# An attention block's instruction order on TensorE: scores ahead of the next rows' transposition; key, values, query in this order

## What is computed

```
x = x + tanh(g_xattn[l]) * attention_l(layernorm(x), ctx, ctx)     # l = 0..3
    scores = Q K^T / sqrt(8);  p = softmax(scores);  out = (p V) Wo + bo
x = x + tanh(g_ffn[l]) * ffn_l(layernorm(x))
```

## Time and profile before

| what | value |
| --- | --- |
| median of 3 runs | 1207.94 us (1206.35 to 1207.98) |
| the profiled execution's own time | 1206.75 us |
| its span, first to last instruction | 1204.6 us |
| PE, DVE, ACT, POOL busy | 78%, 75%, 58%, 44% of the span |
| mean granted TensorE clock over the span | 0.883 of full speed |

### The profile page before, as it was taken

The page is one execution under the profiler, slowest core; times in us unless marked ns, Lnnn a source line. Parts: engine busy times, 40 slices in busy tenths (PEclk is TensorE's granted clock), DMA queues, the critical chain, the costliest instruction groups (busy, mean ns, idle before and its releaser), DMA issues.

```text
span 1204.6 us, 29852 instructions
## 1 busy us (share of the span) xinstructions
PE 936.0 (78%) x11473; PEld 727.7 (60%) x11491; DVE 908.8 (75%) x2195; ACT 693.3 (58%) x1807; POOL 525.5 (44%) x646
## 2 busy tenths in 40 slices
PE   4999979989988860899789999677799998233332
PEld 3888869968876650466377777433488886122221
DVE  3888877857877672566478888688677786999997
ACT  3887754357766620345367777565477876444442
POOL 4444412235477767222478886155523331122222
PEclk9999989999999965899899999788899999556665
DMA  7830000000000001464101100000000000000000
GB/s 203 267 106 2 3 2 2 2 1 2 2 19 25 24 29 48 138 194 140 44 28 28 29 28 20 1 1 1 1 2 2 2 2 2 5 14 13 10 13 17
DMA packets 60526, 44.41 MB, mean 37 GB/s; under 512 B 15197, under 2 KB 55782, under 8 KB 59367
## 3 DMA queue, kind: packets, MB, share of 16 engines
q1 hardware_dynamic: 54996, 33.96, 9.5%
q0 software_dynamic: 4096, 8.34, 2.3%
q10 hardware_dynamic: 1298, 0.27, 0.1%
HBM read 23.73 MB, written 18.87 MB: 35 GB/s over the span
## 4 chain that ended last, share of the span: by engine, by line
issue 38%; PE 30%; DVE 23%; SPq 5%; ACT 2%; POOL 1%; DMA 1%; DVEq 0%; POOLq 0%; another core or an unknown queue 0%; ACTq 0%
PE ps L518 5%; PE ps L547 5%; DVE rowmax L1399 3%; DVE sm L1404 3%; PE ps L585 3%; PE ps L655 2%; PE ps L646 2%; PE ps L647 2%; DVE q_b L1628 2%; DVE q_s L1608 2%; DVE q_r L1619 2%; DVE hT L1598 2%; DVE q_r L1627 2%; PE ps L442 1%; DVE q_r L1566 1%
## 5 line engine op out<-in xcount | busy, mean ns | idle before, releaser
L1399 DVE TENSOR_REDUCE rowmax<-ps 128x16 f32<-128x1024 f32 x128 | 156.7, 1224 | 98.5 <-PE ps L547 98.1
L773 ACT ACTIVATE pr<-ps 128x512 f32<-128x512 f32 x256 | 152.8, 599 | 37.1 <-PE ps L518 35.8
L1404 DVE TENSOR_TENSOR sm<-ps,rowmax 128x1024 f32<-128x1024 f32 x128 | 156.7, 1224 | 3.4
L518 PE MATMUL ps<-cst,sm 128*128 128x128 f32 x1024 | 139.3, 280 | 21.6 <-DVE sm L1404 21.4
L585 PE MATMUL ps<-vbd,pr 128*64 128x18 f32 x4096 | 147.4, 215 | 2.2 <-ACT pr L773 2.2
L585 PEld LDWEIGHTS ps<-vbd,pr 128*64 128x64 f32 x4096 | 134.8, 139 | 15.3 <-ACT pr L773 2.8
L1008 POOL TENSOR_SCALAR xn<-x_sb,mv_all,rstd_all 128x128 f32<-128x128 f32 x128 | 102.2, 799 | 81.4 <-PE ps L524 79.4
L518 PEld LDWEIGHTS ps<-cst,sm 128*128 128x128 f32 x1024 | 113.1, 142 | 31.2 <-DVE sm L1404 30.2
L803 ACT ACTIVATE vbd<-ps 64x128 f32<-64x128 f32 x256 | 71.0, 277 | 92.6 <-PE ps L571 90.4
L807 ACT ACTIVATE qbd<-ps,bqp,cst 128x128 f32<-128x128 f32 x256 | 104.5, 463 | 7.0 <-PE ps L571 3.7
L1075 POOL TENSOR_TENSOR q_out<-q_b,q_s 128x1280 bf16<-128x1280 bf16 (+2 forms) x18 | 38.1, 2119 | 137.5 <-DVE q_b L1629 137.5
(11 more groups left out here) (244 smaller groups left out, 2374.6 us busy)
## 6 DMA issues: line engine op xcount, KB each, us to landing
slots<-hT SPq DMA_DIRECT2D x8, 1024.0 KB, 10.7
sm<-slots SPq DMA_DIRECT2D x32, 256.0 KB, 3.2
expert_out<-xn_all SPq DMA_DIRECT2D x16, 256.0 KB, 2.9
ew<-in_L_ffn_w SPq DMA_DIRECT2D x24, 128.0 KB, 2.5
out<-x_sb SPq DMA_DIRECT2D x32, 64.0 KB, 1.5
slots<-xn_all,row_s POOLq DMA_INDIRECT x64
big<-expert_out,row_g POOLq DMA_INDIRECT x64
x_sb<-in_x SPq DMA_DIRECT2D x1, 512.0 KB, 6.5
```

Source lines behind the costliest of these rows:

```text
L518: last = nc.tensor.transpose(bank(y, b)[:, r * P:(r + 1) * P], sm[y][:, c:c + P], ident)
L773: nc.scalar.activation(pr[y][:, b, :], bank(y, b), ACT.Exp, scale=SCALE).then_inc(p_ready[y], 1)
L1399: v.tensor_reduce(row3, sc, AX.X, ALU.max).then_inc(rowmax_ready[x], 1)
L1404: v.tensor_tensor(sm[x][:, :].rearrange("p (r g k) -> p r g k", r=RG, k=S), sc, row3.unsqueeze(3).broadcast_to([P, RG, 4, S]), ALU.subtrac ...
```

## The change

In TensorE's half the scores of new and the transposition of the output of old come directly behind the eight transpositions; the context or router transposition and that of the rows of ahead come behind them. Then follow the key of ahead, the weight preparation or the router's product, the values of new (now into bank 1 of y, behind the wait for the second exponential), the query of ahead and the products with the probabilities. The wait for `xnT_ready` moves to just ahead of the query; the waits of the output's transposition for `xnT_ready`, `ctxT_ready` and `rT_ready` are gone. ScalarE takes both exponentials first, then waits for the output's, the context's or router's and the rows' transposition, copies the rows, the context or router rows and the output, then the values, and waits for key and query only behind them. VectorE's and GpSimd's programs are not edited.

```
--- before.py
+++ after.py
@@ -517,25 +517,17 @@
                                 c = (2 * r + b) * P
                                 last = nc.tensor.transpose(bank(y, b)[:, r * P:(r + 1) * P], sm[y][:, c:c + P], ident)
                             last.then_inc(smT_psum[y], 1)
-                    if ahead is not None:
-                        if prev is None and k > 0:
-                            pe.wait_ge(x_done[y], IT * k)
-                        pe.wait_ge(xn_ready[y], IT * k + ahead + 1)
-                        nc.tensor.transpose(bank(y, 3)[:, 0:P], xn[y][:, :], ident).then_inc(xnT_psum[y], 1)
-                    if l == 0:
-                        turn_context(t, y)
-                    if l == 1:
-                        turn_routed(t, y)
-                    if old is not None:
-                        pe.wait_ge(o_ready[x], IT * l + old + 1)
-                    if oldest is not None:
-                        pe.wait_ge(x_done[y], IT * k + oldest + 1)
                     if l == 1:
                         reuse_routing_bank(t, x)
                     if new is not None:
                         if prev is not None:
                             pe.wait_ge(v_taken[y], IT * l + prev + 1)
                         pe.wait_ge(k_ready[x], IT * l + new + 1)
+                    if oldest is not None:
+                        pe.wait_ge(x_done[y], IT * k + oldest + 1)
+                    if old is not None:
+                        pe.wait_ge(o_ready[x], IT * l + old + 1)
+                    if new is not None:
                         if l == 1:
                             for r in range(RG):
                                 rows = slice(r % 2 * S, (r % 2 + 1) * S)
@@ -548,27 +540,20 @@
                                                         kT[x][rows, :, b * S:(b + 1) * S], start=(l != 1), stop=True, skip_group_check=True)
                         last.then_inc(s_psum[x], 1)
                     if old is not None:
-                        if ahead is not None:
-                            pe.wait_ge(xnT_ready[y], IT * k + ahead + 1)
-                        if l == 0 and turned_context(t) is not None:
-                            pe.wait_ge(ctxT_ready, turned_context(t) - FIRST + 2)
-                        if l == 1 and routed(t + 1) is not None:
-                            pe.wait_ge(rT_ready[y], routed(t + 1) // NS + 1)
                         nc.tensor.transpose(bank(y, 3)[:, P:2 * P], o_sb[x][:, :], ident).then_inc(oT_psum[x], 1)
-                    if prev is not None:
-                        pe.wait_ge(p_ready[y], 2 * (IT * l + prev) + 1)
-                    if new is not None:
-                        for b in range(2):
-                            for a in range(2):
-                                cols = wv[l][:, :].rearrange("d (r a w) -> d a r w", a=2, w=2 * HD)[:, a, :, :]
-                                dst = bank(y, 0)[a * S:(a + 1) * S, 2 * P + b * S:2 * P + (b + 1) * S].rearrange("p (r w) -> p r w", r=RG)
-                                last = nc.tensor.matmul(dst, ctxT[:, t * P + b * S:t * P + (b + 1) * S], cols, start=True, stop=True, skip_group_check=True)
-                        last.then_inc(v_psum[x], 1)
+                    if l == 0:
+                        turn_context(t, y)
+                    if l == 1:
+                        turn_routed(t, y)
                     if ahead is not None:
-                        if old is None:
-                            pe.wait_ge(xnT_ready[y], IT * k + ahead + 1)
-                        nc.tensor.matmul(bank(y, 0)[:, P:2 * P], wq[l][:, :], xnT[y][:, :], start=True, stop=True)
-                        nc.tensor.matmul(bank(y, 0)[:, 0:P], wk[l][:, :], ctxT[:, (ahead * NS + y) * P:(ahead * NS + y + 1) * P], start=True, stop=True).then_inc(kq_psum[y], 1)
+                        if prev is None and k > 0:
+                            pe.wait_ge(x_done[y], IT * k)
+                        pe.wait_ge(xn_ready[y], IT * k + ahead + 1)
+                        nc.tensor.transpose(bank(y, 3)[:, 0:P], xn[y][:, :], ident).then_inc(xnT_psum[y], 1)
+                    if ahead is not None:
+                        if prev is not None:
+                            pe.wait_ge(p_ready[y], 2 * (IT * l + prev) + 1)
+                        nc.tensor.matmul(bank(y, 0)[:, 0:P], wk[l][:, :], ctxT[:, (ahead * NS + y) * P:(ahead * NS + y + 1) * P], start=True, stop=True)
                     if l == 0:
                         prepare_weights(t, y)
                     if l == 1:
@@ -576,6 +561,17 @@
                     if prev is not None:
                         pe.wait_ge(v_taken[y], IT * l + prev + 1)
                         pe.wait_ge(p_ready[y], 2 * (IT * l + prev) + 2)
+                    if new is not None:
+                        for b in range(2):
+                            for a in range(2):
+                                cols = wv[l][:, :].rearrange("d (r a w) -> d a r w", a=2, w=2 * HD)[:, a, :, :]
+                                dst = bank(y, 1)[a * S:(a + 1) * S, 2 * P + b * S:2 * P + (b + 1) * S].rearrange("p (r w) -> p r w", r=RG)
+                                last = nc.tensor.matmul(dst, ctxT[:, t * P + b * S:t * P + (b + 1) * S], cols, start=True, stop=True, skip_group_check=True)
+                        last.then_inc(v_psum[x], 1)
+                    if ahead is not None:
+                        pe.wait_ge(xnT_ready[y], IT * k + ahead + 1)
+                        nc.tensor.matmul(bank(y, 0)[:, P:2 * P], wq[l][:, :], xnT[y][:, :], start=True, stop=True).then_inc(kq_psum[y], 1)
+                    if prev is not None:
                         for r in range(RG):
                             for h2 in range(2):
                                 for b in range(2):
@@ -775,7 +771,10 @@
                 def half(t, x, fetch, further, later, ahead, new, prev, old, oldest):
                     y = 1 - x
                     if prev is not None:
-                        exponentials(y, 0, 2 * (IT * l + prev) + 1)
+                        for b in range(2):
+                            exponentials(y, b, 2 * (IT * l + prev) + 1 + b)
+                    if old is not None:
+                        act.wait_ge(oT_psum[x], IT * l + old + 1)
                     if l == 0 and turned_context(t) is not None:
                         act.wait_ge(ctxT_psum, turned_context(t) - FIRST + 2)
                     if l == 1 and routed(t + 1) is not None:
@@ -787,22 +786,18 @@
                         empty_context(t, y)
                     if l == 1:
                         empty_routed(t, y)
-                    if prev is not None:
-                        exponentials(y, 1, 2 * (IT * l + prev) + 2)
                     if old is not None:
-                        act.wait_ge(oT_psum[x], IT * l + old + 1)
                         nc.scalar.activation(oT[x][:, :], bank(y, 3)[:, P:2 * P], ACT.Copy).then_inc(oT_ready[x], 1)
-                    if ahead is not None:
-                        act.wait_ge(kq_psum[y], IT * l + ahead + 1)
                     if new is not None:
                         act.wait_ge(v_psum[x], IT * l + new + 1)
                         for a in range(2):
                             part = slice(a * S, (a + 1) * S)
                             dst = vbd[x][part, :].rearrange("p (r a h w) -> p a r h w", a=2, h=2, w=VW)[:, a, :, :, 0:HD]
-                            src = bank(y, 0)[part, 2 * P:3 * P].rearrange("p (r h w) -> p r h w", h=2, w=HD)
+                            src = bank(y, 1)[part, 2 * P:3 * P].rearrange("p (r h w) -> p r h w", h=2, w=HD)
                             last = nc.scalar.activation(dst, src, ACT.Copy)
                         last.then_inc(v_taken[x], 1)
                     if ahead is not None:
+                        act.wait_ge(kq_psum[y], IT * l + ahead + 1)
                         for a in range(2):
                             nc.scalar.activation(qbd[y][:, :, a], bank(y, 0)[:, P:2 * P], ACT.Identity, scale=parity[:, a:a + 1], bias=bqp[l][:, a:a + 1])
                         for a in range(2):
```

## The result

The kernel after takes 1224.24 us (median of 4 runs, 1223.43 to 1233.49), the kernel before 1207.96 beside it: a ratio of 1.013, 95% interval 1.0086 to 1.0174. Slower, by some 16 us; forecast were 1222 and a range of 1210 to 1230. The intervals reach at least 0.35% to each side, so the 0.2% that the prediction takes as what a measurement tells from none was too fine.) Its profiled execution took 1223.87 us against 1206.75, which is +17.1 where the sum had +15.2.

What follows compares the result with a forecast made beforehand. TensorE was taken to bound attentions 3, 0 and early 1, held releases attention 2, with holds also in attention 1's scatter part. Terms 0 + 2.0 + 6.7 + 6.5 + 0 = +15.2 on 1206.75 gave 1222 us, range 1210 to 1230.

Steps and rivals of the forecast that it cites:

- The router's product: Attention 1: it waits for ScalarE's copy of its rows, TensorE stalls 0.58 us a router half; +6.7 before the scatters.
- TensorE's own work: All attentions: nothing added or removed, tile forms change three times as before; 0, ends -1.6 to +4 us.
- The first part of attention 1: Halves before the scatters: 5.2 us from 9 TensorE-bound halves, 0.9 from 4 with routing steps, 0.6 from the last three.
- The scatter part: Last 13 halves of attention 1: same stall, half a us a half taken, +6.5; ends 0 and +12.
- B: Rival: attention 1's scatter halves lock into long ones, +12 there, +20.7 in all, 1227 us; chance 0.18.
- The scores' cover in attention 0: Attention 0: scores start earlier but wait for VectorE's scaled output; 0.9 us in weight halves, 1.1 in bias halves, +2.0.
- Attention 2: Scores end 0.11 earlier, but their release follows the gather's end; 0, ends -3 and +2 us.
- C: Rival: in attention 2 the earlier scores slip out before the gather's hold, -15 us, 1200.5 us in all; chance 0.10.
- A: Rival: attention 1's scatter halves swallow the delay, 0.45 stands for 0.58 elsewhere; +7.5, 1214 us; chance 0.24.
- D: Rival: no real change; tile forms, not order, bound the kernel and the router's copies are early enough; chance 0.06.

Runs made afterwards that it cites:

- router_late: The kernel after with the router's product moved behind the query, ahead of the products with the probabilities: 1207.27 us, ratio 0.998 to the kernel before.

## Why the prediction was right

- *The router's product.* Right in mechanism: it waits for the copy, the label is ScalarE's router copy, and moving it alone takes the loss away. The size was short. Predicted were 0.58 of stall and halves of 5.56; measured 0.66 and 5.70. The copy of the rows of ahead starts 0.39 behind the start of their transposition (300.18 to 300.57). The step had taken 0.31 for this from the earlier trace rows, but there 294.57 is the start of the router's transposition; the rows of ahead had been turned before it, and ScalarE was busy with an exponential until just ahead of 294.88, so the 0.31 measured no hand-over. The other 0.07 no run explains; the sum had put TensorE's own work at 0.
- *The first part of attention 1.* +7.9 undisturbed, against 5.2 + 0.9. The eight halves with nothing but the router's stall gave 5.9 (5.70 to 5.75 instead of 4.97). The four with routing steps on VectorE gave 2.6 where 0.22 each had been counted: the slack that was to absorb the stall there was hardly any. The first five gave 0.5 back.
- *The scatter part.* +6.5 predicted, +7.9 measured. But the step reasoned with holds that may swallow or multiply the delay, and took the middle without a reason of its own, so that it came close is luck. Neither happened: it is 0.6 to 0.7 a half with holds and without. The halves did lock into one length, as B said; the price of that was not there.
- *The scores' cover in attention 0.* +2.0 predicted, +2.4 measured, and the cause shown. The nine weight halves lost 0.19 each on average where 0.10 was taken, so of the 0.22 nearly nothing was slack, and the six bias halves 0.23 to 0.29 instead of 0.16 to 0.22: 3.4 us together. That the window grew by only 2.4 comes from the other halves, which got shorter and were not in the sum.
- *TensorE's own work.* Predicted 0, with an upside of 0.02 a half. Attention 3 gained 0.05, 1.4 us.
- *Attention 2.* Predicted 0; the 0.8 less is inside what the traces scatter. The row maxima are still held on the first chip, with halves of 4.98 us on average, so C fell.
- *Between the stages.* Not in the sum; the 2.3 us less are not shown to come from the change. That the total came out within some 2 us is in good part luck: attention 1 gave +19 instead of +13.2 (1.8 of it by the one half in which the clock was down), attention 0 +2.4, and -4.5 came from what had been put at 0, of which only the 1.4 of attention 3 came again in other traces.
- *The rivals.* A is out (nothing was swallowed), D too. What the forecast had not seen as a case is that the size of the earlier trace rows differs from chip to chip.

## What to carry to other kernels

When work is moved on an engine that issues in order, look first at the smallest instruction that waits: here a product of 8 columns stalled everything behind it for 0.66 us in each router half, and it was cured by putting the values and the query ahead of it. What counts for such a wait is where the copy stands on the engine that makes it, and what the copies ahead of it wait for, not only when its own input is ready. And before a gap is taken as something that a delay could hide in, see whether the gap is there on another chip.

## What the runs showed of the hardware

- While GpSimd issues indirect DMAs, VectorE started 0.59 us and 1.89 us (at 401.27) behind the modelled end of the matmuls it waited for on the first chip; on another it was 0.05, with the same kernel and the same mean duration of a scatter (1.03 us). Traces with such holds came from three groups (the first chip, and those with the kernel before at 1204.67 and 1204.94 us), traces without from two. About 24 us of this kernel's time lie between two such chips (14.1 in attention 1, 10.1 in attention 2). What differs between the chips stays open, and so does whether the scatters are the cause, since the kernel without them never came to a chip with holds.
- With holds, moving one small product behind two others made the scatter part 70.7 us, where the order of before has 82.2 on the same chip with nearly the same work on TensorE. Its products end ahead of the scatters, at 393.96 for instance, and VectorE's denominators wait 2.6 us in all instead of the 17.2 of the kernel before on the first chip. The timeline of the router_late kernel:

```profile
392.82 1.14 PE L581 MATMUL ps<-vbd,pr 128*64 128x18 f32 x32
394.10 1.09 POOL L967 DMA_INDIRECT slots<-xn_all,row_s  x1 [0.18 <-issue]
394.27 0.25 DVE L1342 RECIPROCAL rden<-ps 128x16 f32<-128x16 f32 x1
```

and its group over the 13 halves:

```profile
L1342 DVE RECIPROCAL rden<-ps 128x16 f32<-128x16 f32 x13 | 3.2, 250 | 2.6 <-remote 1.5 <-PE ps L504 0.9
```

- A weight load that waits for a semaphore held back the load behind it, which waited for nothing: the values' load started at 301.38, 0.31 us behind the router's at 301.07.
- The price of a change to a smaller tile form, about 0.20 us, held in the new order: from the key to the values it is 0.42 us (954.71 to 955.13), where a projection alone takes 0.22.
